# Nine reads of scan states on GpSimd instead of four, and new instruction orders on every engine

## What is computed

```
# norm 0: recurrent attention, 16 heads of 8 channels
k = sigmoid(x @ key_w.T + key_b);  v, q = split(x @ vq_w.T)
kv[t] = k[t] * kv[t-1] + (1 - k[t]) * v[t]      # per head an 8 x 8 state, scanned over t
x = layernorm(x + (q . kv) @ out_w.T + out_b)
# norm 1: one expert of 8, chosen by gumbel noise
x = layernorm(x + x @ W[idx] + b[idx])
# norm 2: linear attention through a per-head metric
p = x @ proj;  x = layernorm(x + (((p @ metric) @ p.T) @ p) @ mixer_w.T + mixer_b)
# norm 3: feed-forward, hidden width 512
h = silu(x @ w1 * s1) * (x @ w2 * s2)
h = gelu(h @ h1 * h1s);  h = gelu(h @ h2 * h2s)
x = layernorm(x + h @ w3 * s3)
```

## Time and profile before

| | before |
|---|---|
| median of 3 runs | 193.96 us |
| the profiled execution | 193.92 us |
| its span, first to last instruction | 192.1 us |
| TensorE matmul busy | 173.9 us (91%) |
| VectorE busy | 143.7 us (75%) |
| ScalarE busy | 124.9 us (65%) |
| GpSimd busy | 69.6 us (36%) |
| granted TensorE clock, mean | 0.984 of full speed |

### The profile page before, as it was taken

One profiled execution on the slowest core, in us unless ns is written; L12 is line 12 of the kernel. 1 busy time (PEld: TensorE's weight loads), 2 busy tenths in 40 slices (PEclk: granted clock), 3 DMA queues, 4 the chain that ended last, 5 costly groups with the idle time before them and its releaser, 6 DMA issues. The chain is left out here.

```text
span 192.1 us, 2885 instructions
## 1 busy us (share of the span) xinstructions
PE 173.9 (91%) x949; PEld 138.1 (72%) x949; DVE 143.7 (75%) x371; ACT 124.9 (65%) x207; POOL 69.6 (36%) x65
## 2 busy tenths in 40 slices
PE   7779796999999999999999999999899999999930
PEld 7447483768977788888888899876678775586810
DVE  0799999999999997679979986668470774804461
ACT  3895915963838588648786560577887578975720
POOL 1020002640330662525172740442556336285320
...
DMA packets 6705, 7.85 MB, mean 41 GB/s; under 512 B 544, under 2 KB 5664, under 8 KB 6432
## 3 DMA queue, kind: packets, MB, share of 16 engines
...
HBM read 6.58 MB, written 1.05 MB: 40 GB/s over the span
## 5 line engine op out<-in xcount | busy, mean ns | idle before, releaser
L878 DVE TENSOR_TENSOR_SCAN state<-rep_bank,keep 128x256 f32<-128x256 f32 x62 | 38.6, 672 | 0.0
L347 POOL TENSOR_TENSOR rstd<-varied,power 128x4 f32<-128x4 f32 x15 | 15.9, 1063 | 57.0 <-DVE varied L937 57.0
L1335 PEld LDWEIGHTS y_bank<-attend_pack,read 128*128 128x128 f32 x256 | 31.4, 192 | 4.5 <-issue 2.6
L1335 PE MATMUL y_bank<-attend_pack,read 128*128 128x128 f32 x256 | 32.8, 276 | 0.7 <-DVE read L888 0.3
L585 ACT ACTIVATE hid_even_high<-c_bank,scales_pack 128x512 fp32r<-128x512 f32 x15 | 10.3, 689 | 17.9 <-PE c_bank L1430 17.9
L356 POOL TENSOR_TENSOR hid_odd_low<-hid,hid_odd_high 128x512 fp32r<-128x512 f32 x12 | 15.9, 1323 | 15.2 <-ACT hid L591 15.1
L591 ACT ACTIVATE hid<-c_bank,scales_pack 128x512 f32<-128x512 f32 x31 | 21.2, 684 | 0.0
L888 DVE TENSOR_TENSOR read<-state,query 128x512 f32<-128x512 f32 x28 | 20.8, 754 | 0.0
L1430 PE MATMUL c_bank<-hid_even_high,hidden_rounded 128*128 128x512 f32 x64 | 19.2, 411 | 0.5 <-ACT gate L574 0.5
L1430 PE MATMUL c_bank<-hid_odd_low,hidden_rounded 128*128 128x512 f32 x64 | 18.5, 398 | 0.5 <-DVE hid_odd_low L1033 0.5
L1430 PE MATMUL c_bank<-hid_even_low,hidden_rounded 128*128 128x512 f32 x64 | 18.7, 398 | 0.0
...
## 6 DMA issues: line engine op xcount, KB each, us to landing
...
```

Source lines behind the costliest of these rows:

```text
L347: nc.gpsimd.tensor_tensor(rstd[n][:], varied[n][:], power[:], ALU.pow).then_inc(ln_rstd[n], 1)
L878: ins = nc.vector.tensor_tensor_scan(state[:, e % STATES, at], rep_bank[e % 2][:, at], keep[:, a * T + s * SEQ:a * T + (s + 1) * SEQ], 0.0 ...
L1335: ins = nc.tensor.matmul(y1_bank[:, tile(j)], read[:, e % READS, tile(j)], out_w_rep_sb[:, e, :], start=(e == 0 and j == 0), stop=False, s ...
```

## The change

POOL_READS grows from four to nine entries: (0, 6), (1, 0), (1, 7), (2, 0) and (2, 7) go from VectorE to GpSimd. No instruction is added or taken away beside that, and no helper is changed; the calls of all four compute engines are put in a new order. The core of the diff: GpSimd's first part, ScalarE's first part and group 2's second Gelu layer, VectorE's first part, TensorE's first part and group 2.

```diff
-POOL_READS = ((1, 2), (1, 5), (2, 2), (2, 5))
+POOL_READS = ((0, 6), (1, 0), (1, 2), (1, 5), (1, 7), (2, 0), (2, 2), (2, 5), (2, 7))
...
@@ -377,21 +377,26 @@
 
             constants()
             attend_residual(0)
+            read_state(0, 6)
+            read_state(1, 0)
             inverse_std(0, 0)
+            read_state(1, 2)
             passed_weights()
             attend_residual(1)
-            read_state(1, 2)
+            read_state(1, 5)
             inverse_std(1, 0)
-            read_state(1, 5)
+            read_state(1, 7)
+            read_state(2, 0)
             read_state(2, 2)
+            attend_residual(2)
             inverse_std(2, 0)
             inverse_std(0, 1)
             low_product(0, 0)
+            read_state(2, 5)
             inverse_std(1, 1)
-            read_state(2, 5)
             low_product(0, 1)
-            attend_residual(2)
             low_gelu(0, 1, 0)
+            read_state(2, 7)
             low_gelu(0, 1, 1)
             low_gelu(0, 1, 2)
             inverse_std(2, 1)
...
@@ -620,103 +625,104 @@
             first_high(1)
             first_keep(1)
             cast_rows(1)
+            first_query()
+            projected(3)
+            high_values(0, 1)
             routing(0)
-            first_query()
+            projected(4)
             routing(1)
+            projected(5)
             routing(2)
-            high_values(0, 1)
             routing(3)
-            projected(3)
-            projected(4)
+            high_values(1, 0)
+            projected(6)
+            copy_proj_metric()
+            sum_low_halves(0)
+            high_values(1, 1)
+            projected(7)
             round_weights(0)
-            high_values(1, 0)
-            projected(5)
-            sum_low_halves(0)
             sum_low_halves(1)
-            high_values(1, 1)
-            projected(6)
-            projected(7)
+            high_values(2, 0)
             projected(8)
-            copy_proj_metric()
+            sum_low_halves(2)
+            norm_out(0, 0)
+            move_x1(0)
+            round_weights(1)
             projected(9)
-            norm_out(0, 0)
+            silu_table(1)
             projected(10)
-            move_x1(0)
-            silu_table(1)
-            round_weights(1)
-            high_values(2, 0)
+            silu_table(2)
             norm_out(1, 0)
             move_x2(0)
-            move_heads(0)
             projected(11)
             high_values(2, 1)
+            move_heads(0)
             move_mixed(0)
-            sum_low_halves(2)
-            round_weights(2)
             norm_out(2, 0)
             high_x3(0)
             norm_out(0, 1)
+            high_values(3, 0)
             silu(0, 0)
...
             whole_gelu(2, 1, 0)
-            move_mixed(3)
             high_gelu(2, 1, 1)
             whole_gelu(2, 1, 1)
             high_gelu(2, 1, 2)
             whole_gelu(2, 1, 2)
+            keep_residual(2)
+            move_mixed(3)
             high_gelu(2, 1, 3)
             whole_gelu(2, 1, 3)
             high_gelu(2, 2, 0)
             whole_gelu(2, 2, 0)
+            silu_table(3)
             high_gelu(2, 2, 1)
             whole_gelu(2, 2, 1)
+            high_x3(3)
             high_gelu(2, 2, 2)
             whole_gelu(2, 2, 2)
             high_gelu(2, 2, 3)
             whole_gelu(2, 2, 3)
-            high_x3(3)
             silu(3, 0)
             narrow_out(2)
             high_product(3, 0)
@@ -761,13 +767,12 @@
             high_product(3, 1)
             silu(3, 3)
             high_product(3, 2)
-            silu_table(3)
             high_product(3, 3)
             high_gelu(3, 1, 0)
             whole_gelu(3, 1, 0)
-            keep_residual(3)
             high_gelu(3, 1, 1)
             whole_gelu(3, 1, 1)
...
@@ -1044,162 +1049,156 @@
             first_scan(1)
             scan(0, 1)
             scan(0, 2)
+            low_values(0, 1)
             read_state(0, 0)
             scan(0, 3)
-            low_values(0, 1)
-            route_on(0)
             read_state(0, 1)
             scan(0, 4)
+            value_steps(1)
+            route_on(0)
+            read_state(0, 2)
             route_on(1)
-            read_state(0, 2)
+            scan(0, 5)
+            read_state(0, 3)
             route_on(2)
-            read_state(0, 3)
-            value_steps(1)
+            low_values(1, 0)
             route_on(3)
             read_state(0, 4)
-            scan(0, 5)
-            low_values(1, 0)
             scan(0, 6)
             route_on(4)
+            read_state(0, 5)
             scan(0, 7)
-            read_state(0, 5)
             route_on(5)
-            read_state(0, 6)
             direct_product(0)
             read_state(0, 7)
+            route_on(6)
             scan(1, 0)
+            low_values(1, 1)
             scan(1, 1)
-            route_on(6)
             norm_sum(0, 0)
-            low_values(1, 1)
+            value_steps(2)
             norm_stats(0, 0)
             norm_moments(0, 0)
             route_on(7)
             norm_varied(0, 0)
-            read_state(1, 0)
+            read_state(1, 1)
             scan(1, 2)
             norm_shift(0, 0)
-            value_steps(2)
             scan(1, 3)
-            read_state(1, 1)
+            scan(1, 4)
             read_state(1, 3)
-            scan(1, 4)
+            scan(1, 5)
             norm_sum(1, 0)
             norm_stats(1, 0)
             norm_moments(1, 0)
+            read_state(1, 4)
             norm_varied(1, 0)
-            scan(1, 5)
+            scan(1, 6)
             norm_shift(1, 0)
-            scan(1, 6)
+            low_values(2, 0)
             scan(1, 7)
-            read_state(1, 4)
-            direct_product(1)
-            low_values(2, 0)
             read_state(1, 6)
             scan(2, 0)
+            scan(2, 1)
+            direct_product(1)
+            low_values(2, 1)
             mask_gram(0)
-            read_state(1, 7)
-            scan(2, 1)
-            read_state(2, 0)
+            read_state(2, 1)
+            value_steps(3)
+            scan(2, 2)
             residual_of_metric(0)
-            scan(2, 2)
-            read_state(2, 1)
+            norm_sum(0, 1)
             norm_sum(2, 0)
             norm_stats(2, 0)
             norm_moments(2, 0)
-            top_remainder()
             norm_varied(2, 0)
-            norm_sum(0, 1)
-            rounding_flag()
             norm_stats(0, 1)
             norm_shift(2, 0)
             norm_moments(0, 1)
-            low_values(2, 1)
+            top_remainder()
             norm_varied(0, 1)
+            scan(2, 3)
             direct_product(2)
-            scan(2, 3)
             norm_shift(0, 1)
+            rounding_flag()
             low_x3(0)
+            read_state(2, 3)
             scan(2, 4)
-            read_state(2, 3)
             read_state(2, 4)
             product(0, 0)
-            product(0, 1)
...
@@ -1551,74 +1551,75 @@
                 first_project(0, 0)
                 first_project(1, 0)
                 first_project(0, 1)
+                first_project_query()
                 first_project(1, 1)
-                first_project_query()
                 first_replicate(0)
                 first_replicate(1)
                 replicate(0, 1)
+                project(3)
                 replicate(0, 2)
-                project(3)
                 replicate(0, 3)
                 project(4)
+                project(5)
                 attend(0, 0)
                 replicate(0, 4)
+                replicate(0, 5)
+                project(6)
+                replicate(0, 6)
+                attend(0, 1)
                 sum_query(0)
-                replicate(0, 5)
-                attend(0, 1)
-                replicate(0, 6)
-                project(5)
+                replicate(0, 7)
+                project(7)
                 attend(0, 2)
                 attend(0, 3)
+                project_metric()
                 attend(0, 4)
-                replicate(0, 7)
-                project(6)
+                attend(0, 5)
                 replicate(1, 0)
-                replicate(1, 1)
-                attend(0, 5)
                 attend(0, 6)
                 attend(0, 7)
+                replicate(1, 1)
                 attend_direct(0)
+                project(8)
+                sum_query(1)
+                project(9)
                 replicate(1, 2)
                 replicate(1, 3)
-                project(7)
-                project_metric()
-                project(8)
-                project(9)
+                attend(1, 0)
+                project(10)
                 replicate(1, 4)
-                project(10)
+                replicate(1, 5)
                 transposes(0, 0)
-                attend(1, 0)
+                attend(1, 1)
                 routed(0)
-                project(11)
-                attend(1, 1)
-                replicate(1, 5)
```

(69 more changed lines are left out.)

179 lines of the change are left out of this document (87 added, 92 removed).

## The result

The changed kernel takes 195.22 us (median of 20 runs, 193.45 to 196.93), the kernel before 194.22 beside it; the ratio is 1.005, interval 1.0026 to 1.0073. It is slower by half a per cent, where the forecast was 193.5 with "no change" likeliest. The ratio leaves out the executions in a slower state, three of the changed kernel's twenty (196.62 to 196.93 us), and the medians do not.

What follows compares the result with a forecast made beforehand. VectorE's queue was taken to bound the first third, a full TensorE the rest from the feed-forward layers on. 193.92 - 0.7 - 0.3 + 0.6 = 193.5 us, own range 192.6 to 194.6, with rivals 191.2 to 195.7.

Steps and rivals of the forecast that it cites:

- The reads: Before the feed-forward layers: a moved read gives VectorE back 0.58 us, but waits leave the layers starting as before.
- Rival A: The added waits do not arise, feed-forward layers start 1.7 us earlier, table loads are hidden: 191.7 us, chance 0.27.
- Rival B: SBUF lock before 58 us: whichever of GpSimd and VectorE starts second waits; two hits give 195.4 us, chance 0.10.
- Term 1: Up to hidden(0, 1, 0): low halves 0.4 us later, but TensorE has done 1.1 us more work: -0.7 us.
- Term 2: At 132 us: up_of(2, 0) behind narrow(1) covers TensorE's wait for narrow_out(1); the wait before heads_of(3) stays: -0.3 us.
- Term 3: Group 2's second Gelu layer: silu_table(3) brings two more table loads on ScalarE, partly covered: +0.6 us, bounds 0 and 2.8.
- The clock is no term: Granted clock is 1.00 (2.4 GHz) in all three stretches and TensorE stays as busy, so nothing was added for it.
- Rival C: Group 2's second Gelu layer: the table loads stand open in full, 195.7 us, chance 0.15.
- D: No table load comes with silu_table(3), as order alone doesn't tell where loads are put: 192.9 us, chance 0.05.
- The lock's rule: Two SBUF inputs on VectorE against a GpSimd operation reading SBUF: first to issue wins; scans and sums from PSUM are free.

Runs made afterwards that it cites:

- e17: Kernel before with three more reads, (0, 6), (1, 0) and (2, 0), on GpSimd, all else kept, measured a second time; ratio 0.997 (0.994 to 1.001).
- e8: Kernel before with the five reads moved to GpSimd, nine there in all, and every other order kept; ratio 1.011 (1.005 to 1.016).
- e1: Changed kernel with silu_table(3) back behind all Gelus of group 2, so without the two extra table loads; median 198.2 us, no ratio.
- e9: Changed kernel with top_remainder and rounding_flag early again, around norm_varied(2, 0), as in the kernel before; ratio 1.007 (1.004 to 1.010).
- e5: Changed kernel with silu_table(3) behind group 2's Gelus and GpSimd's low_gelu(2, 2, 1) held until norm_out(2, 3) is complete; ratio 1.004 (1.000 to 1.008).

## Why the prediction was wrong, by its steps

**The reads.** The price of a moved read held (e17's scan behind the moved read (0, 6) began 0.52 us earlier, for 0.58 forecast; on GpSimd a read took 1.42 us in the changed kernel's mean, as three of nine took 1.63, 1.72 and 1.77), and so did the step that most of it is turned into waits: sum at 51.88 for 51.8 forecast, shift 55.23 for 55.0, flag 57.67 for 57.8, first matmul 58.98 for 58.9. Rival A's waits that "do not arise" did arise. Rival B was right in its rule but not in its place: no VectorE read before 58 us took over 1.2 us in the changed kernel, its order had kept them apart; e8, without that order, lost 1.1 us (1.0 from high_x3(0)), most of it to two collisions.

**Term 1, forecast -0.7.** hidden(0, 1, 0) started 0.76 us later from the first scan (71.16 against 70.23 in the two spans), 0.97 later from high_x3(0), with 1.1 us of work more behind it: -0.4 by the first count, -0.2 by the second, which repeats better. The step that failed is "it holds if TensorE then stays full": it did, nearly (63.85 of 64), yet at transposes(3, 0), with the same work done, the changed kernel is behind (128.13 and 127.65): by 0.3 us from the first scan, by 0.52 from high_x3(0), as in every trace with these orders and no fall (70.64 and 70.65 against 70.08 to 70.13). At through_metric(2), also behind the same work, it is already 0.53 behind. So some 0.7 us went between hidden(0, 1, 0) and that point, where the trace shows TensorE no wait above 0.1 us, and where exactly I can't say. A busy TensorE did not mean equal progress.

**Term 2, forecast -0.3.** The wait for narrow_out(1) went and heads_of(3) waits 0.48 for 0.62, but routed(3) waits 0.35 us for move_x1(3), which the prediction had not followed. At hidden(2, 2, 0) terms 1 and 2 together stand at -0.2 (147.83 with the 0.81 us of metric_out(3) still to do, against 148.71, less the first scans), forecast -1.0. Counted from high_x3(0) they stand at 0.0, behind a start that is 0.1 earlier in the mean.

**Term 3, forecast +0.6.** From there to the end it is +1.0, by either count. The size was off, inside the bounds, and the reason was half seen. The prediction said that the transposes "need a norm that ends at about the same time" as the late Gelu; it did not draw the conclusion, that hidden(2, 2, 3) is then late by 1 us whichever of the two ends first. It also took a load on ScalarE as only a cost; here it kept GpSimd off the norm (e1).

**The clock.** "The clock is no term" failed, and it is the step that no part of the sum allowed for. Half of the traces of the new order pay 1.3 us (e9 1.0), two of nine of the old pay 1.3. Without a fall the change costs 1.00 from high_x3(0) less 0.1 for the earlier start: 0.9. On the mean that is 0.9 + 0.5 x 1.28 - 0.22 x 1.31 = 1.25 us, beside 0.97 measured (0.5 to 1.4); with so few traces the two shares are rough. One trace without the fall could not have shown it, and the earlier trace rows could not either.

**Which step weighed most.** The forecast had -0.4 us, the runs show about +1.0. Terms 1 and 2 account for 0.9 of the difference (forecast -1.0, found -0.1), term 3 and the clock for about 0.4 each, together 0.3 more than the medians show and inside the interval. So the lead that moved reads and earlier work were to give is the largest failure, and its mechanism is only in part shown: the waits took the place of the reads as forecast, and the loss between hidden(0, 1, 0) and through_metric(2) is open.

**Rival C** (the loads open in full, 195.7) came nearest in time for a reason that was only partly its own; D fell, the loads came.

**The lock's rule.** The prediction took from the Trainium skill ("SBUF — State Buffer", Who interferes with whom) the part on two SBUF inputs. The same section gives a second case, a VectorE operation in a 2-port mode. The traces bear on it: norm_out, with one tensor input, took 2.79 us beside GpSimd in e1 and 1.12 in e5, where GpSimd was held back. The kernel before already had this, with no wait on TensorE behind it, as its transposes stand later:

```profile
152.87 2.58 POOL L356 TENSOR_TENSOR hid_even_low<-hid,hid_even_high 128x512 fp32r<-128x512 f32 x2
...
152.94 3.11 DVE L957 TENSOR_SCALAR normed_lent<-normed_lent,moments,rstd 128x128 f32<-128x128 f32 x4 [0.83 <-POOL rstd L347]
```
